# A mixture-of-experts stage in units of 128 rows, four to a group, instead of 256 rows, two to a group

## The reference, cut to what matters

```
x = x + attention_a(layernorm(x))
x = x + moe(layernorm(x))
x = x + attention_b(layernorm(x))
x = x + moe(layernorm(x))
```

## Time and profile before

| | us |
|---|---|
| median of 3 runs | 1403.18 |
| lowest, highest | 1398.74, 1406.71 |
| the profiled execution | 1396.88 |
| its span, first to last instruction | 1395.1 |
| TensorE busy | 1239.1 (89%) |
| VectorE busy | 1042.0 (75%) |
| GpSimd busy | 836.4 (60%) |
| ScalarE busy | 756.4 (54%) |

### The profile page before, as it was taken

The page is one execution under the profiler, slowest core; times in us unless marked ns, Lnnn a source line. Parts: engine busy times, 40 slices in busy tenths (PEclk is TensorE's granted clock), DMA queues, the critical chain, the costliest instruction groups (busy, mean ns, idle before and its releaser), DMA issues.

```text
span 1395.1 us, 28372 instructions
## 1 busy us (share of the span) xinstructions
PE 1239.1 (89%) x8534; PEld 787.4 (56%) x8534; DVE 1042.0 (75%) x4462; ACT 756.4 (54%) x1901; POOL 836.4 (60%) x1246
## 2 busy tenths in 40 slices
PE   3999998996999999999999999999999999999100
PEld 1566665565898965454545445545455469888100
DVE  2899999895674458898999989989998856565322
ACT  2444444442665767666676756656676546556000
POOL 3237776777525224356777767766874445367776
PEclk9999999997999998998999989999999899999655
DMA  6845602011556520000100001011000125466522
GB/s 174 259 154 192 197 30 87 28 44 60 171 163 210 166 65 16 14 11 24 32 25 29 32 24 32 29 62 48 29 28 14 44 79 162 150 218 205 150 75 75
DMA packets 119783, 125.80 MB, mean 90 GB/s; under 512 B 15568, under 2 KB 109904, under 8 KB 119632
## 3 DMA queue, kind: packets, MB, share of 16 engines
q1 hardware_dynamic: 103248, 90.42, 20.5%
q0 software_dynamic: 16384, 33.59, 7.9%
HBM read 50.15 MB, written 73.79 MB: 89 GB/s over the span
## 4 chain that ended last, share of the span: by engine, by line
PE 70%; DVE 12%; POOL 7%; issue 4%; DMA 2%; ACT 2%; SPq 0%; POOLq 0%; ACTq 0%; DVEq 0%
PE pair L1897 25%; PE pair L1823 8%; POOL vmyg L564 6%; PE pair L1685 5%; DVE pT L1401 5%; PE bank L1709 4%; PE pair L1834 4%; PE pair L1812 2%; PE bank L1630 2%; PE bank L1624 2%; PE pair L1674 2%; DVE xs L1318 2%; PE bank L1936 1%; PE bank L1916 1%; PE pair L1695 1%
## 5 line engine op out<-in xcount | busy, mean ns | idle before, releaser
L1897 PE MATMUL pair<-kT,apart 32*128 32x512 f32 x2048 | 460.2, 672 | 3.5 <-DVE smax L1401 2.0
L1401 DVE CUSTOM_DVE_ANT_0 pT<-pair,pT 128x256 f32<-128x256 f32 x1024 | 384.2, 416 | 76.1 <-ACT pT L925 70.4
L925 ACT ACTIVATE pT<-pair 128x256 f32<-128x256 f32 x1024 | 327.0, 397 | 196.8 <-PE pair L1897 193.3
L1897 PEld LDWEIGHTS pair<-kT,apart 32*128 32x128 f32 x2048 | 192.8, 192 | 128.1 <-DVE smax L1401 78.7
L564 POOL DMA_INDIRECT vmyg<-ybufA,slg x128 | 123.7, 966 | 110.6 <-DVE smax L1401 67.9
L1823 PE MATMUL pair<-xeT,unit_w 128*128 128x256 f32 x768 | 184.6, 384 | 0.0
L564 POOL DMA_INDIRECT vmyg<-ybufB,slg x128 | 122.8, 959 | 71.3 <-DVE smax L1401 33.6
L509 POOL DMA_INDIRECT dispB<-xnf,sli x128 | 129.3, 1010 | 57.0 <-issue 35.2
L509 POOL DMA_INDIRECT dispA<-xnf,sli x128 | 130.0, 1016 | 50.9 <-issue 30.2
L1128 DVE TENSOR_TENSOR pT<-pair,causal 128x1024 f32<-128x1024 f32 x128 | 151.2, 1213 | 12.1 <-PE pair L1685 11.2
L1293 DVE TENSOR_TENSOR hid<-sg,pair 128x512 f32<-128x512 f32 x96 | 65.7, 685 | 123.3 <-ACT sg L851 123.1
(11 more groups left out here) (231 smaller groups left out, 1947.6 us busy)
## 6 DMA issues: line engine op xcount, KB each, us to landing
dispB<-zeros SPq DMA_DIRECT2D x16, 1408.0 KB
apart<-dispA SPq DMA_DIRECT2D x96, 128.0 KB
ybufA<-ye SPq DMA_DIRECT2D x48, 256.0 KB
apart<-dispB SPq DMA_DIRECT2D x96, 128.0 KB
ybufB<-ye SPq DMA_DIRECT2D x48, 256.0 KB
dispA<-zeros SPq DMA_DIRECT2D x33, 128.0 KB
xs<-in_x SPq DMA_DIRECT2D x16, 256.0 KB, 3.1
out<-xs SPq DMA_DIRECT2D x15, 256.0 KB, 2.6
```

The costliest lines, as they stand in the source:

```text
L925: act.activation(rel[n % RING][:, q, :], pair[n % RING][:, q, HALF:SEQ], ACT.Relu).then_inc(s["relu_done"], 1)
L1401: dve.tensor_tensor_reduce(out=rel[n % RING][:, q, :], in0=pair[n % RING][:, q, 0:HALF], in1=rel[n % RING][:, q, :], scale=1.0, scalar=LOW ...
L1897: pe.matmul(pair[n % RING][:, q, :], apart[h][at, j, t * P:(t + 1) * P], kTs[h][at, HALF:], start=True, stop=True).then_inc(s["bsc_done"], 1)
```

## The change

A unit is one tile of 128 rows, and a group has four units, so it still has 512 rows and four tiles. 8192 / 128 = 64 units and up to 15 more are rounded up to 80; a stage has 20 groups. Each group has four table entries, four loads, four weight blocks, and gate and up matmuls of 128 columns. The ring of weights has three groups (`NW`) instead of four; its place is counted over all stages. GpSimd copies the first three groups of each stage, ScalarE the others. The scratch `whose` is cut to what half a layer uses. The routing pieces of the last batch in stage 2 and its sends are moved one or two groups earlier.

```diff
--- before.py
+++ after.py
@@ -25,12 +25,13 @@
 CAP = -(-T * K * 5 // (E * 4))
-UT = 2
+UT = 1
...
 SPAN = K * CAP + UR
-GU = 2
+GU = 4
...
 NX = 4
+NW = 3
...
@@ -82,7 +83,7 @@
         f_w = sb("f_w", [P, E, 3 * D])
-        unit_w = [sb(f"unit_w{r}", [P, GU, 3 * D]) for r in range(NX)]
+        unit_w = [sb(f"unit_w{r}", [P, GU, 3 * D]) for r in range(NW)]
...
@@ -190,7 +191,7 @@
         apart = [sb(f"apart{h}", [P, GH, SEQ]) for h in range(2)]
-        whose = sb("whose", [P, NT * K, E])
+        whose = sb("whose", [P, HALFB * TB * K, E])
...
@@ -579,12 +580,12 @@
                     pool.wait_ge(s["w_in2"], 16 * 11)
-                if at >= NX:
-                    pool.wait_ge(s["y_done"], at - NX + 1)
+                if at >= NW:
+                    pool.wait_ge(s["y_done"], at - NW + 1)
...
                 for u in range(GU):
-                    last = pool.tensor_copy(unit_w[g % NX][:, u, :], f_w[:, bass.ds(ex[u], 1), :].rearrange("p a n -> p (a n)"))
+                    last = pool.tensor_copy(unit_w[at % NW][:, u, :], f_w[:, bass.ds(ex[u], 1), :].rearrange("p a n -> p (a n)"))
...
@@ -603,7 +604,7 @@
                 if not next:
-                    for g in range(NX):
+                    for g in range(NW):
...
@@ -749,8 +750,8 @@
             places(B - 1, 2 * B - 1, 1)
-            send_beside(2 * B - 1, B - 1, 1, 17)
-            for g in range(NX):
+            send_beside(2 * B - 1, B - 1, 1, 15)
+            for g in range(NW):
...
@@ -853,9 +854,9 @@
-                    act.wait_ge(s["y_done"], base + g - NX + 1)
+                    act.wait_ge(s["y_done"], base + g - NW + 1)
                     for u in range(GU):
-                        last = act.activation(unit_w[g % NX][:, u, :], f_w[:, bass.ds(ex[u], 1), :].rearrange("p a n -> p (a n)"),
+                        last = act.activation(unit_w[(base + g) % NW][:, u, :], f_w[:, bass.ds(ex[u], 1), :].rearrange("p a n -> p (a n)"),
...
@@ -864,7 +865,7 @@
                     silu(g)
-                    if 2 <= g < G - 2:
+                    if NW - 2 <= g < G - 2:
...
@@ -982,7 +983,6 @@
                     turned(2 * B - 1, "ffn", xfT)
-                if g == 14:
...
@@ -1556,20 +1556,20 @@
                     table_slots(2, (g - 11,))
+                if g == 13:
+                    route_max(b + B, bank[0])
                 if g == 14:
-                    route_max(b + B, bank[0])
+                    route_top(b + B)
                 if g == 15:
-                    route_top(b + B)
+                    route_ranks(b + B, bank[0])
                 if g == 16:
-                    route_ranks(b + B, bank[0])
+                    table_counts(3, bank[0])
                 if g == 17:
-                    table_counts(3, bank[0])
-                if g == 18:
...
                     table_rows(3)
+                if g == 18:
+                    table_copy(3, bank[0])
                 if g == 19:
-                    table_copy(3, bank[0])
-                if g == 20:
...
@@ -1813,11 +1813,11 @@
                 def gate_up(g):
-                    h, r = g % 2, g % NX
+                    h, r = g % 2, (base + g) % NW
                     pe.wait_ge(s["xeT_ready"], g + 1 + base)
-                    pe.wait_ge(s["unit_w_ready"], NX * seg + min(g, NX - 1) + 1)
-                    if g >= NX:
-                        pe.wait_ge(s["unit_w_act"], seg * (GRP - NX) + g - NX + 1)
+                    pe.wait_ge(s["unit_w_ready"], NW * seg + min(g, NW - 1) + 1)
+                    if g >= NW:
+                        pe.wait_ge(s["unit_w_act"], seg * (GRP - NW) + g - NW + 1)
...
@@ -2070,21 +2070,21 @@
                     scatter_context(b)
-                if g == 13:
+                if g == 12:
...
                     turn(b + B, "ffn", xnf[(b + B) % NF])
-                if g == 14:
+                if g == 13:
                     logits(b + B, bank[0])
-                if g == 16:
+                if g == 15:
...
                     ranks(b + B, bank[0])
-                if g == 17:
+                if g == 16:
...
                     counts(3, bank[0])
-                if g == 19:
+                if g == 18:
...
```

## The result

The changed kernel takes 1431.36 us (median of four runs, 1426.66 to 1438.32) against 1401.33 us before: a ratio of 1.0214, 95% interval 1.0186 to 1.0242, so slower by some 30 us. The profiled execution took 1430.19 us, its span 1428.4.

What follows compares the result with a forecast made beforehand. It took TensorE to bound the expert stages before, and SP's 4.49 us turn after. Terms of +1.9, +0.1, +15.3 and +27.1 sum to +44.4, 1441.3 to 1447.6 by scale; forecast 1444 us, own range 1430 to 1458, whole range 1412 to 1464.

Steps and rivals of the forecast that it cites:

- its own signs: In the new profile: store to store 4.4 to 4.6 us, table reads near 0.87, TensorE idling before down, gathers awaiting indices.
- SP decides: Expert stages: SP's turn per group, now with four loads, outgrows the break-even of 3.67 us and sets the pace.
- The link through `ye`: Before down: with two `ye` buffers, down waits for copy and landed store, keeping TensorE within about two turns of SP.
- The turn, 4.49: SP's turn per group: 2.55 us, plus 1.54 for two more units, plus 0.40 for a longer table read.
- the rival with a flat read: SP's table read doesn't grow with its values: turn 4.09, +20 us, 1417 to 1423 us; chance 0.20.
- Ahead of stage 0, +1.9: Before the first expert stage: GpSimd's first weight copies take 6.7 us against 4.8, delaying ScalarE's norm, +1.9 us.
- Stage 0, +0.1: First expert stage: SP's pace gives 82.3 us against 82.2, with the batch chain that stretched it now hidden.
- Stage 1, +15.3: Second expert stage: no loads made early, so SP's turns give 93.4 us against 78.1.
- The end, +27.1: Third and fourth stages: gathers begin at 107.3 instead of 96.8, wait for indices; ninth batch at 205.3 against 178.2.
- The sum: Whole kernel: all terms together +44.4 us, 1441.3 on the profiled execution's scale, 1447.6 on the median's.
- TensorE's pace, 1376: Rival: TensorE still sets the pace, 11.2 us less in each of the first two stages, 1376 us; chance 0.05.
- ScalarE: Rival: ScalarE's 4.4 us chain per group falls behind too, lengthening stages one and three, 1456 to 1462 us; chance 0.14.

Runs made afterwards that it cites:

- the control: The kernel before, with the range tests of its two table values taken off SP's turn: 1400.0 us, ratio 1.0004.
- four buffers: The changed kernel with four output buffers `ye` for the down product instead of two: 1421.16 us, ratio 1.0153.
- the second profile: The changed kernel run once more with nothing changed, to look at attention B: 1432.5 us, ratio 1.0202.

## Why the prediction was right, and which term was off

It was right in direction, range and mechanism, and 13 us too high. That it came so near is in part luck: its terms add up to 20 us too much, and attention B, which it put at nothing, gave 9.1 of them back in the profiled pair. Of its own signs the waits before down came, released by the copy into `ye` (10.3 us in stage 1, but in 8 of its groups and not in each), and waits for indices; store to store (3.92, not 4.4 to 4.6), the table read (0.30, not 0.87) and stage 1 (83.9, not 90 to 95) missed, all three by the same term. By its own steps:

- **SP decides.** Shown in both directions: turns of 2.88, 3.92 and 4.97 us gave a stage 1 of 71.3, 83.9 and 104.0 us, and the control shows that 2.55 us was harmless in the first two stages before. The link through `ye` was as described, but four buffers show that it was where the lateness appeared, not its cause.
- **The turn, 4.49.** The step that failed is the size of the table read, "0.20 a value, so four take 0.87". The two rows that it rested on the earlier trace rows were right, but the line through them doesn't go on: three values cost 0.985 in the median, four that begin at a multiple of four 0.302. The turn was 3.92, even under the 4.09 of the rival with a flat read. The other terms of the turn, 0.77 a unit, fitted.
- **Ahead of stage 0, +1.9.** +2.0 was measured, yet from GpSimd's first copy to the first transposes only 0.8 of it (26.47 us against 25.64); the twelve copies took 5.6 us, not 6.7. The control, with the old units, began at 344.2, so such a difference can't be told here.
- **Stage 0, +0.1.** -1.7. With a turn of 3.92 SP's pace alone would give less, 73 us by the step's own sum, so something else still holds this stage; that it is the batch chain, which the step put under SP's pace, is argued and not shown.
- **Stage 1, +15.3.** +5.6. The read alone is 0.57 us a turn less, 11 us in 20 turns, a little more than the 9.7 that are missing.
- **The end, +27.1.** +18.2. SP's first load came 87.0 us after 1145.73, the end of stage 2's first transposes, so SP was free near 85.5 (87 taken, bounds 83 and 89); ScalarE's eviction did stand behind four copies, 2.80 us on TensorE. From there the cheaper turn brought the first gather to 103.9 on that scale instead of 107.3, and the waits for the indices were as described, 13.6 us between the first two of them, but shorter in sum.
- **The sum.** +24.1 in the stages, against +44.4 forecast and the +20 of the rival with a flat read: in its sum, in stage 1 and at the end that rival was nearer, in stage 0 and ahead of it the forecast was. The two profiles differ by 33.3 us with attention B's 9.1, the medians by 30; the second profile has +32.4 in the same stages. In both, TensorE's granted clock in stages 2 and 3 is lower than before (0.96 and 0.93, 0.92 and 0.89, against 0.98 and 1.00), the point that the prediction named as making it too low. How much of the time the clock took there was not tried.
- **TensorE's pace, 1376.** Without SP's tests that rival's condition was met, and the whole was 1393.6, not 1376. The first two stages gave back 15.7 us of its 22.4, since its price took TensorE as busy without a break and it was for 91% and 95% of them; the last part stayed 2 us longer than before; and the largest piece of the gap in the profiles, 8.1 us, is attention B (635.2 us against 627.1).
- **ScalarE.** Its chain was put at 4.4. In the run without SP's tests silu to first copy took 1.13 us in the median of stage 1 and 1.43 where the queue's read began with the silu (451.17 and 451.28), not 2.3, since the queue reads and tests the table while the engine still works; with 1.67 for four copies and about 0.5 for xT that is 3.3 to 3.6.

By the floor that the Trainium skill, "DMA: Bandwidth & Descriptors", section "Latency and other measured facts", states, the read would be 0.60 and the time, as an estimate, about 1428, near the result by its total; but no row shows such a floor. 0.27 to 0.31 us were measured for one value and for four that begin at a multiple of four.

## What to carry to other kernels

When units are made smaller, count what the issuing queue pays per unit (read, test, address, DMA) and hold the sum against the engine that sets the pace: a queue with half a microsecond to spare can become the bound. An engine's wait for a buffer that a DMA frees doesn't tell whether latency or the queue's pace is at fault; more buffers tell it, because with a pace the wait only moves. And a gain ahead of a chain at the end, here gathers that take 10 us a batch, came out only when the next gate moved too: the earlier stores gave nothing by themselves, and the earlier sums behind them shortened the last part by another six microseconds.

## What the runs showed of the hardware that was not expected

- A read of table values into registers is not linear: in the median 0.28, 0.47 and 0.985 us for one, two and three values, 0.30 for four that begin at a multiple of four, and 1.38 for four that don't (0.86 to 1.62 over both runs with such reads). The Trainium skill, "Runtime: NRT & Kernel Launch", section "Instruction fetch mechanics", gives about 200 ns a register; the trace agrees for the second value (0.19) and for the cheapest reads of three, not for their median and not for the four at 0.30.
- VectorE's two index copies of 128x8 took 4.84 us at 1230.07 while GpSimd made twelve copies of weights (1229.82, 5.45 us); before they took 0.23 (1209.70). The Trainium skill, "SBUF — State Buffer", section "SBUF: two separate sides", says that a pair of ports shared by the two engines is an exclusive lock, held for a whole instruction by a GpSimd operation or by a VectorE operation of certain kinds. The trace fits as far as the eleventh copy: the first index copy lasts until that one ends (4.77 us), and no gap between the eleven let it in; the second, 0.16 us, lies beside the twelfth, which the trace doesn't explain. It cost nothing here, since SP's stores came later still.
